# Decoder layer on one core: cross-attention scores as row tiles of the array, softmax steps over a whole token tile

## The reference

```python
q = split_heads(queries @ Wq + bq)          # 16 heads of 16
k = split_heads(keys @ Wk + bk)             # 64 keys
v = split_heads(values @ Wv + bv)
scores = jnp.einsum('bhqd,bhkd->bhqk', q, k) / jnp.sqrt(jnp.float32(HD))
scores = jnp.where(mask, jnp.float32(-1000000000000000.0), scores)
attn = jax.nn.softmax(scores, axis=-1)
ctx = jnp.einsum('bhqk,bhkd->bhqd', attn, v)
ctx = ctx.transpose(0, 2, 1, 3).reshape(b, sq, d)
return ctx @ Wo + bo
...
x = _layernorm(x + attention(x)); x = _layernorm(x + cross_attention(x)); x = _layernorm(x + experts(x))
```

## Time and profile before

| what | value |
|---|---|
| median of 3 runs | 716.82 us (715.99 to 722.28) |
| the profiled execution's own time | 716.99 us |
| its span, first to last instruction | 715.3 us |
| outside the span | 1.7 us |
| granted TensorE clock, mean of the span | 0.949 of 2.4 GHz |
| PE busy / DVE / ACT / POOL | 85% / 66% / 49% / 44% |
| middle part | about 354 to 517 us |

### The profile page before, as it was taken

One profiled execution on the slowest core, in us unless ns is written; L12 is line 12 of the kernel. 1 busy time (PEld: TensorE's weight loads), 2 busy tenths in 40 slices (PEclk: granted clock), 3 DMA queues, 4 the chain that ended last, 5 costly groups with the idle time before them and its releaser, 6 DMA issues.

```text
span 715.3 us, 12852 instructions
## 1 busy us (share of the span) xinstructions
PE 610.7 (85%) x3820; PEld 369.4 (52%) x3820; DVE 469.3 (66%) x1304; ACT 351.5 (49%) x735; POOL 316.6 (44%) x393
## 2 busy tenths in 40 slices
PE   5888899999999998998799997958646888888884
PEld 3434434434434342254377774834436777777741
DVE  0369878888788883069478874736325756767657
ACT  1312376666676667816375442413223545555543
POOL 8413312234332442547666163545474454554530
PEclk9989999999999999999999996979867999999988
DMA  5867766337165300049000021111354664566756
GB/s 165 169 169 148 159 211 93 67 50 99 30 80 81 44 4 18 18 146 372 1 1 0 1 73 56 64 64 57 120 160 142 201 203 138 152 208 198 240 200 212
DMA packets 52113, 82.51 MB, mean 115 GB/s; under 512 B 11936, under 2 KB 29600, under 8 KB 51744
## 3 DMA queue, kind: packets, MB, share of 16 engines
q1 hardware_dynamic: 45184, 62.26, 35.6%
q0 software_dynamic: 6864, 19.44, 7.4%
HBM read 53.38 MB, written 32.48 MB: 120 GB/s over the span
## 4 chain that ended last, share of the span: by engine, by line
PE 62%; DVE 17%; another core or an unknown queue 6%; ACT 4%; issue 4%; DMA 3%; POOL 2%; SPq 1%; DVEq 0%; ACTq 0%; POOLq 0%
PE ps L1480 9%; PE ps L1745 9%; PE ps L1456 8%; PE ps L1439 7%; DVE neg_max L922 5%; PE ps L1768 4%; PE ps L1643 3%; PE ps L1662 3%; PE ps L1724 2%; PE ps L1788 2%; PE ps L1757 2%; PE ps L1588 2%; PE ps L1444 2%; PE ps L1652 2%
## 5 line engine op out<-in xcount | busy, mean ns | idle before, releaser
L922 DVE TENSOR_REDUCE neg_max<-ps 128x1 f32<-128x512 f32 (+3 forms) x304 | 181.9, 655 | 43.1 <-PE ps L1444 26.6
L775 ACT ACTIVATE temps<-ps 128x1024 f32<-128x1024 f32 (+1 forms) x192 | 147.5, 812 | 78.1 <-PE ps L1456 78.0
L674 POOL TENSOR_SCALAR_AFFINE_SELECT temps<-temps 128x256 f32<-128x256 f32 x128 | 52.2, 411 | 148.1 <-ACT temps L775 147.2
L1439 PE MATMUL ps<-stacks 96*128 96x512 bf16 (+3 forms) x384 | 105.4, 331 | 11.6 <-DMA stacks<-qk_parts 5.1
L745 POOL DMA_INDIRECT expert_outputs<-x_T,w_o_xqkv x79 | 76.6, 970 | 74.3 <-ACT x_T L895 37.5
L1456 PE MATMUL ps<-stacks 99*128 99x512 bf16 (+3 forms) x384 | 93.3, 328 | 2.9 <-DMA stacks<-m_rows 1.4
L1480 PE MATMUL ps<-temps,v_group 128*32 128x512 f32 (+3 forms) x768 | 81.8, 497 | 1.6 <-POOL temps L674 1.0
L1745 PE MATMUL ps<-w_split,block_x 128*128 x474 | 73.0, 291 | 5.8 <-DVE block_x L1327 2.9
L738 POOL DMA_INDIRECT expert_slots<-x_tok,w_o_xqkv x64 | 62.4, 974 | 28.7 <-issue 17.2
L1745 PEld LDWEIGHTS ps<-w_split,block_x 128*128 128x128 f32 x474 | 64.2, 196 | 7.4 <-issue 7.2
L1456 PEld LDWEIGHTS ps<-stacks 99*128 99x128 bf16 x384 | 26.9, 97 | 75.1 <-ACT temps L775 49.6
(11 more groups left out here) (213 smaller groups left out, 1092.6 us busy)
## 6 DMA issues: line engine op xcount, KB each, us to landing
stacks<-qk_parts SPq DMA_DIRECT2D x96, 128.0 KB, 5.7
v_group<-expert_slots SPq DMA_DIRECT2D x79, 138.5 KB
qk_parts<-temps SPq DMA_DIRECT2D x8, 768.0 KB, 4.4
w_raw<-in_w SPq DMA_DIRECT2D x4, 1024.0 KB, 10.4
early_parts<-expert_outputs SPq DMA_DIRECT2D x4, 1024.0 KB
expert_slots<-in_pad SPq DMA_DIRECT2D x16, 138.5 KB
expert_slots<-in_pad SPq DMA_DIRECT2D x1, 2077.5 KB
x_T<-in_xT SPq DMA_DIRECT2D x4, 512.0 KB, 7.4
```

Of the source, the lines that this page charges most:

```text
L674: nc.gpsimd.affine_select(diag, diag, [[0, 2], [1, P]], ALU.is_ge, zero, base=0, channel_multiplier=-1).then_inc(b_cut, 1)
L775: nc.scalar.activation(pt[:, n % 4, :, 0:w], ps[:, 2 + 2 * (n % 2):4 + 2 * (n % 2), 0:w], ACT.Exp, scale=SCALE).then_inc(b_exp, 1)
L922: nc.vector.tensor_reduce(nmx[:, c, h0:h0 + nh, i], ps[:, A_BANKS[n % 3], 0:w * nh].rearrange("p (h k) -> p h k", h=nh), axis=AX.X, op=ALU ...
L1439: last = nc.tensor.matmul(ps[:, A_BANKS[n % 3], w * s:w * s + w], qs[0:KR, ua, h0 + s, P * i:P * i + P], ks[0:KR, ua, h0 + s, CH * c:CH * ...
```

## The change: what it does

S is done once for a token tile, in the pass of its first half. The 16 heads' scores are eight multiplications of 32 rows by 128 columns: for each half o, four of them in the four row groups of the array (rows 32q to 32q + 31, two heads each), each writing its own bank q of banks 0 to 3, columns 128 o to 128 o + 127. The mask follows as four multiplications of 256 columns. DVE takes one maximum and one subtraction of 1024 columns for the tile; ACT still takes two exponentials, each over four runs of 128 columns.

So that S can have four banks, T has one bank (4) in place of two, V's two halves go to banks 5 and 6 beside the transposes and the projection, and the ranks' columns move. T waits until the previous half's transposes are copied (`xpT_kept`, n, not n - 1). The first half's V waits for N of the tile before, as it did, and now also for O (`xo_kept`) and, after K, for I (`r_index`). `LAGS` is written in another order: within a pass Y (for PE) comes first, then V, N, P, O, T, and S comes after Z, X, L, R, Q and W; a new kind F carries DVE's share of the old Y. The shared expert's first multiplications wait for the last subtraction.

```diff
-LAGS = {"S": 0, "T": 2, "V": 4, "N": 4, "P": 5, "O": 5, "Y": 6, "Z": 7, "X": 8, "L": 9, "R": 9, "Q": 10,
-        "W": 11, "K": 12, "I": 12}
+LAGS = {"Y": 6, "V": 4, "N": 4, "P": 5, "O": 5, "T": 2, "F": 6, "Z": 7, "X": 8, "L": 9, "R": 9, "Q": 10, "W": 11,
+        "S": 0, "K": 12, "I": 12}
...
                 if kind == "S":
-                    act.wait_ge(xs_sub, n + 1)
+                    act.wait_ge(xs_sub, n // 2 + 1)
                     if n >= 2:
                         act.wait_ge(xpT_ready, n - 1)
-                    nc.scalar.activation(px[:, n % 2, :], sx[:, n % 2, :], ACT.Exp, scale=SCALE).then_inc(xp_exp, 1)
+                    nc.scalar.activation(px[:, n % 2, :].rearrange("p (q s) -> p q s", q=4),
+                                         sx[:].rearrange("p o s -> p (o s)").rearrange("p (q o s) -> p q o s", q=4, o=2)
+                                         [:, :, n % 2, :], ACT.Exp, scale=SCALE).then_inc(xp_exp, 1)
...
                 if kind == "S":
-                    s3 = ps[:, n % 2, :].rearrange("p (h k) -> p h k", h=8)
-                    dve.wait_ge(xs_ready, n + 1)
-                    nc.vector.tensor_reduce(mxx[:, n % 2, :], s3, axis=AX.X, op=ALU.max).then_inc(xs_max, 1)
...
+                    if n % 2 == 0:
+                        t = n // 2
+                        s4 = ps[:, 0:4, 0:2 * P].rearrange("p q (h k) -> p q h k", k=S2)
+                        m3 = mxx[:].rearrange("p o h -> p (o h)").rearrange("p (q h) -> p q h", q=4)
+                        dve.wait_ge(xs_ready, t + 1)
+                        nc.vector.tensor_reduce(m3, s4, axis=AX.X, op=ALU.max).then_inc(xs_max, 1)
+                        dve.wait_ge(xs_max, t + 1)
+                        wait(dve, xp_exp, n)
...
                 if kind == "N":
-                    heads = ps[:, 4, 0:H * VW].rearrange("p (h v) -> p h v", h=H)
+                    heads = ps[:, 5:7, D:D + H // 2 * VW].rearrange("p o (h v) -> p o h v", v=VW)
                     dve.wait_ge(xo_ready, 2 * n + 2)
+                    wait(dve, xo_kept, n)
...
-                if kind == "Y":
+                if kind == "F":
                     dve.wait_ge(y_ready, NT + n + 1)
...
-                    nc.tensor.matmul(ps[:, n % 2, :], q2[:, o, P * t:P * t + P],
-                                     kbd[:, o, t // TB].rearrange("p h k -> p (h k)"), start=True, stop=False)
-                    nc.tensor.matmul(ps[:, n % 2, :], identb[:], mask[:, t, :].unsqueeze(1).to_broadcast([P, 8, S2]),
-                                     start=False, stop=True).then_inc(xs_ready, 1)
+                    if n % 2 == 0:
+                        t = n // 2
+                        wait(pe, xs_sub, t)
+                        for o in range(2):
+                            for q in range(4):
+                                rows = slice(32 * q, 32 * q + 32)
+                                nc.tensor.matmul(ps[:, q, P * o:P * o + P], q2[rows, o, P * t:P * t + P],
+                                                 kbd[rows, o, t // TB, 2 * q:2 * q + 2].rearrange("p h k -> p (h k)"),
+                                                 start=(o == 0), stop=False, skip_group_check=True)
+                        for q in range(4):
+                            last = nc.tensor.matmul(ps[:, q, 0:2 * P], identb[:],
+                                                    mask[:, t, :].unsqueeze(1).to_broadcast([P, 4, S2]),
+                                                    start=False, stop=True, skip_group_check=True)
+                        last.then_inc(xs_ready, 1)
...
                 if kind == "T":
                     pe.wait_ge(xp_exp, n + 1)
-                    if n >= 2:
-                        pe.wait_ge(xpT_kept, n - 1)
+                    wait(pe, xpT_kept, n)
...
                 if kind == "V":
                     t, o = n // 2, n % 2
                     pe.wait_ge(xpT_kept, n + 1)
-                    if o == 0 and t >= 1:
-                        pe.wait_ge(xo_norm, t)
+                    if o == 0:
+                        wait(pe, xo_norm, t)
+                        wait(pe, xo_kept, oT_turned[0])
+                        wait(pe, r_index, ranked[0])
+                    else:
+                        taken[0] = t + 1
                     for r in range(4):
-                        at = 2 * VW * (4 * o + r)
-                        last = nc.tensor.matmul(ps[:, 4, at:at + 2 * VW], pTx[:, n % 2, r, :],
+                        at = D + 2 * VW * r
+                        last = nc.tensor.matmul(ps[:, 5 + o, at:at + 2 * VW], pTx[:, n % 2, r, :],
```

48 lines of the change are left out of this document (22 added, 26 removed).

## The result

The changed kernel took **740.86 us** (median of 4 runs, 738.71 to 746.05), the kernel before beside it 716.40 (706.51 to 722.28): ratio 1.040, 95% interval 1.028 to 1.052. The forecast was 722.8 with a range of 713 to 738, so it was too low, and the range's upper end too. The profiled execution had 740.38 us, its span 738.6.

The account below looks back on a forecast made before the run. The prediction took a full PE to bound the kernel before and a loop through DVE's softmax the new one. Its terms, -0.8 + 5.7 + 4.0 - 2.9 = +6.0 us, gave 722.8 us, range 713 to 738.

Parts of the forecast that it names:

- Scores on PE: PE's work per tile: four row groups run at once, scores take 0.70 us, masks 0.43, PE falls from 6.07 to 5.04.
- Rival (a): Scores on PE: the row groups do not run at once, the loop becomes 7.0 us, 738 us in all; chance 0.12.
- Softmax on DVE: DVE's 1024-column pair: 1.27 us, then 1.43 up to N's multiplication; 3.12 us from the maximum's start to N's end.
- The loop that decides: Steady tile: first-half V waits for N behind the pair, so a tile goes from 6.07 to 6.0 us; -0.8 us.
- x: Time of a tile's scores on PE: 0.70 us including entering and leaving the divided array, bounds 0.43 and 1.71.
- The first tiles: Start of the stage: each first T precedes the next S, so the fourth S comes 16.4 us after the first; +5.7 us.
- The routing: First two groups' routing: longer waits around Q, W and I add 2.3 and 1.7 us; +4.0 us together.
- What takes some of it back: Half-clock stretch after PE's pause at 428 to 437 us: the new kernel loses less there; -2.9 us.
- Rival (d): Steady tiles: PE, busy 5.04 of 6.0 us, falls to half the clock, 12 x 2.8 = +34, 751 us; chance 0.04.
- Rival (b): PE's pause after a group's scatters swallows the delay that the routing adds; 717 to 719 us; chance 0.18.

Follow-up runs that it names:

- e6: Changed kernel with scores multiplied over all 128 rows of the array instead of 32; tile 7.20 us, first S to first block 16.3 us longer than a0's.
- e1: Changed kernel with PE's waits in the first tiles filled by unused identity multiplications; ratio 1.034 to the kernel before, first S to first block 166.6 us.
- b0: The kernel before, unchanged, profiled again in the other kind of session; first S to first block 143.8 us.
- a0: The changed kernel, unchanged, run again in the other kind of session; ratio 1.036 to the kernel before, first S to first block 166.9 us.
- e11: Changed kernel with K and I (the ranks and what is read from them) at the front of their pass on every engine; ratio 1.017 to the kernel before.
- e4: Changed kernel with the ranks in bank 7 behind the logits instead of bank 5 behind V's first half; ratio 1.033 to the kernel before.
- e5: Changed kernel with S first in each pass on every engine, as in the kernel before; ratio 1.10, a plain tile 10.3 to 11 us.
- e8: e1 plus idle identity multiplications ahead of the last transposition in each later tile; ratio 1.026 to the kernel before.
- e2: e1 plus 12 idle multiplications ahead of the first three groups' ranks; first S to first block as long as a0's.
- e12: e11 and e8 together, with 6 instead of 14 idle multiplications in the first group's tile; ratio 1.017 to the kernel before.
- e16: e11 with the first tiles' waits filled, and three idle multiplications only in tiles that no routing touches; ratio 1.028 to the kernel before.
- e3: Changed kernel with S first in its pass on PE alone and the first tiles' waits filled with idle multiplications; ratio 1.007 to the kernel before.

## Why the prediction missed

**Scores on PE: right.** 0.66 us, and 0.09 on the transposition ahead of them for entering the divided array, together 0.75 against 0.70; the masks 0.44 against 0.43. Rival (a), had it been true, would have cost what e6 cost: 16.3 us in the middle, where the forecast said 15.

**Softmax on DVE: right.** 384.43 - 383.17 = 1.26 and 385.85 - 384.43 = 1.42, against 1.27 and 1.43.

**The loop that decides: right**, 6.18 us against 6.0, with a gap of 0.88. The excess: 0.11 us from N's end to V instead of 0.05, V 0.88 instead of 0.81, and 0.53 from T to the scores instead of 0.44 (entering the divided array, a price that I had put into x). The gap is put down to "issue" here, not to N as I had said; that it is N is worked out from its end at 386.27, and two tiles earlier, at 371.60, the profile does name N (0.83 us).

**The first tiles: the mechanism right, the clock left out.** 16.4 us stood for the full clock, and at the full clock it is 16.9 (e1). But the kernel itself took 21.2, since after the 3.24 us of waiting PE ran at 1.2 GHz. The step costed each instruction at its full-clock row.

**The routing: the step that failed.** It said +2.3 and +1.7 us. In b0 and a0 the groups' stretches lost 5.0, 6.7 and 1.8, the clock's share among them. In the first session's changed kernel the tenth and eleventh tile took 19.8 us, 7.4 more than two plain tiles, where the forecast had 5.0 and the kernel before 2.7. W itself took the 2.7 us that I gave it (416.17 to 418.87), and V waited for I as forecast. Missing is a wait that the change adds: the ranks' for `xo_norm` (3.06, 1.02 and 1.29 us in a0). I had W "stand before the maximum" and let V wait for I, and did not ask who waits for W now and what else it waits for. e11 takes this wait and V's for I away together, and its middle is 7.1 us shorter; e4, which takes away V's alone, gains nothing in the middle, since the ranks then wait longer. The change had moved V's first half into the bank of the ranks. With the order as it is this costs some 7 us, where the cheaper scores gained nothing in a steady tile (6.18 us against 6.07).

**What takes some of it back: not seen.** The -2.9 us rested on one half-clock stretch of the kernel before. The third stretch, where it lies, lost 7.0 us in the first session, and 6.7 in the one where the kernel before had no such stretch. The working had a slip as well: a tile at half the clock was put at 8.8 us, though PE's own 5.04 us become 10.1 there. e5's tiles at half the clock take 10.3 to 11 us. Rival (d), 12 x 2.8, is too small for the same reason. Rival (b), by which the pause would swallow the delay, falls with the same two losses.

**The second step that failed: the clock, put at nothing in the sum.** It stood in rival (d) alone, with a chance of 0.04 and in a wrong place. (d) looked at steady tiles alone, found them at a busy share of 5.04 of 6.0, and took the earlier trace rows of the kernel before as evidence, though PE was then full. In the changed kernel the steady tiles held (one fell in e1), and the clock fell first behind the longest waits (3.24 us before 358, 3.07 before 422). Over the middle it was at half for 55 us longer in the first session and 37 in the second. At 0.29 us each from e8 that is 16 and 11 us, a rough estimate, of 24 and 23, since the rate varies (e2, e12); e8 itself won back 8.7. What the forecast lacked was the length: no term of its sum has the clock fall at a new place. Of the 17 us that it lacks in the middle (23.1 against 6.0), some 4 lie ahead of the first logits (9.6 against 5.7 less 0.3 of plain tiles) and 13 behind them.

**What stays open.** The clock and the ranks' wait overlap: each alone gives 7 to 9 us in the middle (e11, e8), both together 8.9 in e12 and 7.7 in e16. Why taking one away lets the other's loss return as half clock in other tiles was not settled, nor why the clock falls in e3 with PE full. Nor is it parted what of the 7 us is the ranks' wait and what V's for I. And e16's third stretch still takes 32.4 us against 27.3 before, without an experiment of its own.

## What to carry to other kernels

When a full engine is given less work, what it waits for becomes the tile: cost the new loop, and then every wait of that engine that the diff adds, one by one, asking for each what is queued ahead of the instruction it waits on. Price PE's waits twice: once as time, and once as a stretch at half the clock behind them, for all of the places where PE now stands still, not only the typical tile. And filling PE's waits with idle work is a good probe of the clock and an unsure remedy: it won 6 to 9 us in e8 and nothing in e1 and e2, and at half the clock the fill takes twice as long and stands in the way.
